# A fused attention and feed-forward kernel: linear-attention and expert weights split in the attention groups and kept in DRAM, all second butterfly stages on GpSimd

## The reference, cut to what matters

```python
x = x + xattn(layernorm(x), ctx, wq, wk, wv, wo, ...)     # 4 batches x 4 kv heads = 16 groups
def h_bitlinear(x, w):                                    # the feed-forward: gate, up, down
    return act_quant(fwht(x)) @ weight_quant(w).T         # weights become -1, 0, 1 times mean(|w|)
x = x + h_bitlinear(silu(h_bitlinear(n, w_gate)) * h_bitlinear(n, w_up), w_down)
x = x + linear_attention(layernorm(x), ctx, Wq, Wg, bg, Wkv, Wo)
x = x + experts(layernorm(x), router_gate, expert_gate_up, expert_down)
```

## Time and profile before

| | |
|---|---|
| median of 3 runs | 1307.87 us (1306.95 to 1311.53) |
| the profiled execution | 1307.24 us, of which the span of the trace is 1305.4 us |
| PE busy | 1194.1 us (91%) |
| DVE busy | 1017.2 us (78%) |
| ACT busy | 839.2 us (64%) |
| POOL busy | 796.9 us (61%) |
| transfers | 157.06 MB, 120 GB/s on average |
| chain that ended last | PE 71%, DVE 13%, DMA 5%, POOL 4%, ACT 3% |

### The profile page before, as it was taken

The page is one execution under the profiler, slowest core; times in us unless marked ns, Lnnn a source line. Parts: engine busy times, 40 slices in busy tenths (PEclk is TensorE's granted clock), DMA queues, the critical chain, the costliest instruction groups (busy, mean ns, idle before and its releaser), DMA issues.

```text
span 1305.4 us, 30426 instructions
## 1 busy us (share of the span) xinstructions
PE 1194.1 (91%) x11547; PEld 895.8 (69%) x11547; DVE 1017.2 (78%) x1971; ACT 839.2 (64%) x1920; POOL 796.9 (61%) x1020
## 2 busy tenths in 40 slices
PE   4998699999999999999999999999999775689898
PEld 2554487777777787877777777777778554466557
DVE  6876778888787887878887888888788577796763
ACT  4665577776667777666767676776777463347431
POOL 2775486775858586675858576685858374452100
PEclk9998999999999999999999999999999887799899
DMA  8630268658866767786575857656676967000000
GB/s 285 199 96 1 35 128 153 138 134 149 172 134 132 146 127 144 139 177 145 124 148 119 153 130 142 136 135 134 133 142 130 193 156 166 1 1 1 1 1 33
DMA packets 499938, 157.06 MB, mean 120 GB/s; under 512 B 484801, under 2 KB 493777, under 8 KB 499793
## 3 DMA queue, kind: packets, MB, share of 16 engines
q1 hardware_dynamic: 497664, 147.77, 53.8%
q0 software_dynamic: 2128, 7.35, 2.1%
HBM read 29.12 MB, written 4.33 MB: 26 GB/s over the span
## 4 chain that ended last, share of the span: by engine, by line
PE 71%; DVE 13%; DMA 5%; POOL 4%; issue 3%; ACT 3%; SPq 0%; POOLq 0%; DVEq 0%; ACTq 0%
PE PS L1179 14%; PE PS L1181 13%; PE PS L1180 13%; PE PS L1331 8%; PE PS L1327 7%; PE PS L1328 7%; DVE mx L1684 4%; DMA pT_l<-pl 3%; DVE pl L1704 2%; PE PS L1280 2%; DMA pT_h<-ph 2%; PE PS L693 1%; DMA sin<-in_c_sin 1%; PE PS L668 1%; PE PS L1289 1%
## 5 line engine op out<-in xcount | busy, mean ns | idle before, releaser
L1684 DVE TENSOR_REDUCE mx<-PS 128x1 f32<-128x512 f32 (+2 forms) x512 | 297.0, 622 | 137.0 <-PE PS L1181 135.4
L1327 PE MATMUL PS<-v_h,pT_h 128*128 128x129 f16 (+1 forms) x1856 | 228.6, 223 | 14.0 <-DMA pT_h<-ph 13.9
L1328 PE MATMUL PS<-v_l,pT_h 128*128 128x128 f16 (+1 forms) x1856 | 228.5, 222 | 0.0
L1922 POOL CAST ph<-pr_end 128x705 f16<-128x705 f32 (+1 forms) x128 | 109.2, 853 | 176.0 <-ACT pr_end L1479 170.1
L1327 PEld LDWEIGHTS PS<-v_h,pT_h 128*128 128x128 f16 (+1 forms) x1856 | 184.1, 99 | 18.3 <-DMA pT_h<-ph 15.5
L1179 PE MATMUL PS<-kT_h,qT_h 128*128 128x512 f16 (+2 forms) x512 | 182.4, 356 | 7.3 <-ACT pr L1479 7.3
L1328 PEld LDWEIGHTS PS<-v_l,pT_h 128*128 128x128 f16 (+1 forms) x1856 | 184.3, 99 | 2.5
L1479 ACT ACTIVATE pr<-PS,nb 128x1024 f32<-128x1024 f32 x128 | 143.9, 1124 | 65.3 <-DVE nb L1692 65.2
L1181 PE MATMUL PS<-kT_h,qT_l 128*128 128x512 f16 (+2 forms) x512 | 181.7, 355 | 0.0
L1180 PE MATMUL PS<-kT_l,qT_h 128*128 128x512 f16 (+2 forms) x512 | 181.7, 355 | 0.0
L1704 DVE TENSOR_TENSOR pl<-pr,ph 128x1024 f16<-128x1024 f32 x128 | 173.1, 1353 | 0.0
(11 more groups left out here) (301 smaller groups left out, 2961.7 us busy)
## 6 DMA issues: line engine op xcount, KB each, us to landing
stage<-in_ctxT SPq DMA_DIRECT2D x8, 800.5 KB, 6.8
lanes<-in_w_lanes SPq DMA_DIRECT2D x16, 192.0 KB, 3.7
stage<-in_wq SPq DMA_DIRECT2D x4, 512.0 KB, 3.9
stage<-in_wo SPq DMA_DIRECT2D x4, 512.0 KB, 3.7
pT_h<-ph SPq DMA_TRANSPOSE x128, 3.6
pT_l<-pl SPq DMA_TRANSPOSE x128, 3.6
ctx_kept<-ctx_h SPq DMA_DIRECT2D x2, 800.5 KB, 8.1
ctx_kept<-ctx_l SPq DMA_DIRECT2D x2, 800.5 KB, 8.6
```

Source lines behind the costliest of these rows:

```text
L1327: mm(PS[:, OB, 0:DH + 1], pT_h[0:rows, slot, t, :], v_h[0:rows, par, v, :], start=t == 0, stop=False)
L1328: mm(PS[:, OB, 0:DH], pT_h[0:rows, slot, t, :], v_l[0:rows, par, v, :], start=False, stop=False)
L1684: dve.reduce_max(mx[:, c:c + 1], PS[:, c, 0:cols(u % LT, c)], AX_X).then_inc(mx_part, 1)
L1922: pool.tensor_copy(ph[:, slot, HALF:LAST + w], pr_end[:, 0:BANK + w]).then_inc(pool_hi, 1)
```

## The change

The nine blocks that are split into halves leave the last group. In each of groups 0 to 14 SyncE loads one piece of 512 columns (after unit 3), ACT makes its high half (after unit 4), DVE its low half (after unit 5), and SyncE stores both in DRAM (after unit 7). `lanes` and the piece share one buffer, `relay`, so the lane load moves behind unit 0 of the next group and waits for the stores; the strips are 1093 columns wide instead of 1024, fifteen instead of sixteen. After the last group eight transfers bring the halves back, and `linear_q` and `linear_gate` wait for them. The router's weights are loaded whole and split on DVE. Of the six ternary blocks DVE makes three in units 1 to 3 of the last group and three in the tail (`wu`, `wd`); their loads are spread over the end of group 14 and the last group; the mean is made at the end of group 14 and the start of the last. The first output tile of the last group is projected, and the first half rotated and quantised, ahead of the last `pv` on PE and the last `out_norm` on DVE. All second butterfly stages are GpSimd's (`bp`), and the four tail lists have a new order.

```diff
-LANE_N = FF * D // LANES // NG
+LANE_N = -(-LANE_ALL // (NG - 1))
+KEPT = 512
+PIECE_HI_AT, PIECE_LO_AT = 4, 5
-LAST_JOBS_AT = [[("out", 0), ("out", 1)], [("out", 2), ("out", 3), ("weight", 0), ("weight", 1)], ...
+LAST_JOBS_AT = [[("mean", 1), ("out", 0), ("out", 1)], [("out", 2), ("out", 3)], [], [], [], [], [], []]
+TERNARY_AT = {1: 0, 2: 1, 3: 2}
 TAIL_PE = stages("""
-    tr0:00 tr0:01 rot:00 rot:01 tq:00 tq:01 ga0:00 tr0:10 up0:00 ga0:01 tr0:11 up0:01 rot:10 ga0:02
+    tr0:00 tr0:01 rot:00 rot:01 tq:00 tq:01 ga0:00 up0:00 ga0:01 tr0:10 ga0:02 up0:01 rot:10 tr0:11
...
 TAIL_DVE = stages("""
-    st0:00 st0:01 lo0:00 lo0:01 qm:00 qq:00 st0:10 st0:11 hh:00 lo0:10 hh:01 lo0:11 b2:00 qm:10 hh:02
-    qq:10 hh:03 b2:02 hl0:00 hh:10 ...
+    st0:00 st0:01 lo0:00 lo0:01 qm:00 qq:00 st0:10 wu:00 wd:00 st0:11 hh:00 lo0:10 wd:01 hh:01 lo0:11
+    hh:02 qm:10 hh:03 qq:10 hl0:00 hl0:01 hh:10 ...
 TAIL_POOL = stages("""
-    rs0:00 rs0:01 rs0:10 rs0:11 b1:00 b1:01 bp:01 b1:02 b1:03 bp:03 b1:10 b1:11 bp:11 b1:12 b1:13 bp:13
+    rs0:00 rs0:01 rs0:10 rs0:11 b1:00 bp:00 b1:01 b1:02 bp:01 bp:02 b1:03 b1:10 bp:03 bp:10 b1:11 b1:12
+    bp:11 bp:12 b1:13 bp:13 rs1:00 ...
@@ SyncE
             def group(g, last=False):
                 for u in range(UNITS):
                     turn(g, u)
-                    if u == LANE_AT + 3 and not last:
+                    if u == 0 and 0 < g < NG - 1:
+                        lane_load(g)
+                    if u == LANE_AT + 1 and g < NG - 1:
                         sp.wait_ge(lane_sum, g + 1)
-                        sp.dma_start(lanes[:, 1:], w_lanes[:, ds((g + 1) * LANE_N, LANE_N)]).then_inc(lane_in, 16)
+                        sp.dma_start(piece_f.rearrange(...), kept_sources[g]).then_inc(pw_in, 16)
+                    if u == UNITS - 1 and g < NG - 1:
+                        sp.wait_ge(pw_lo, g + 1)
+                        for k, t in enumerate((piece_h, piece_l)):
+                            sp.dma_start(kept_w[k, :, g * KEPT:(g + 1) * KEPT], t).then_inc(pw_kept, 16)
+            def lane_load(g):
+                n = lane_width(g)
+                wait(sp, pw_kept, 32 * g)
+                sp.dma_start(lanes[:, 1:1 + n], w_lanes[:, g * LANE_N:g * LANE_N + n]).then_inc(lane_in, 16)
+            def bring_weights():
+                sp.wait_ge(pw_kept, 32 * (NG - 1))
+                ...
+                        sp.dma_start(t, kept_w[k, :, at * KEPT:(at + n) * KEPT]).then_inc(pw_back, 16)
@@ PE, last group, ahead of the last pv; then after it
                         turn(0, 0, 0)
                         turn(0, 0, 1)
+                        wait_bank(pe, ("out", 2), NG - 2)
+                        out_proj(0, NG - 1, job_bank(("out", 0)))
+                        pe.wait_ge(tw_const, 64)
+                        rotate(0, 0)
+                        rotate(0, 1)
                     pv(g, u, par)
...
-            pe.wait_ge(tw_lo, NTL)
             pe.wait_ge(tw_made, 1)
-            for n, (kind, i) in enumerate(OUT_JOBS):
...
+            turn_first(0, 0)
+            turn_first(0, 1)
+            for i, before in ((1, (("out", 3), NG - 2)), (2, (("out", 0), NG - 1)), (3, (("out", 1), NG - 1))):
+                wait_bank(pe, *before)
+                out_proj(i, NG - 1, job_bank(("out", i)))
             tail()
@@ ACT and DVE, each group but the last
+            def weight_piece_hi(g):
+                act.wait_ge(pw_in, 16 * (g + 1))
+                copy(piece_h, piece_f, WS).then_inc(pw_hi, 1)
+            def weight_piece_lo(g):
+                dve.wait_ge(pw_hi, g + 1)
+                dve.scalar_tensor_tensor(piece_l, piece_f, WS, piece_h, ALU.mult, ALU.subtract).then_inc(pw_lo, 1)
@@ DVE, last group
+                    if last and u == UNITS - 1:
+                        lo_part(0, 0, 0)
+                        lo_part(0, 0, 1)
+                        out_lo_part(0, NG - 1, job_bank(("out", 0)))
+                        quantise(0, True)
+                        quantise(0, False)
+                    out_norm(g, u)
+                    if last and u in TERNARY_AT:
+                        ternary(TERNARY_AT[u], tern, tw_made_ternary)
@@ GpSimd
-                    for i in range(STAGES):
-                        weight_load(i)
+                    if g == NG - 2 and u == UNITS - 2:
+                        pool.wait_ge(kq_lo, NG * KQ_STEPS)
+                        ternary_load(0)
+                    if g == NG - 2 and u == UNITS - 1:
+                        ternary_load(1)
+                    if last and u == 0:
+                        ternary_load(2)
...
+                    if last and u == 2:
+                        ternary_load(3)
+                    if last and u in (4, 5):
+                        ternary_load(u)
@@ PE in the tail
             def up_first(hf, j):
+                if j == 0:
+                    pe.wait_ge(tl["wu"], nth("wu", 0, 0))
             def down_first(hf, j):
+                pe.wait_ge(tl["wd"], nth("wd", 0, 1))
             def linear_q(hf, k):
+                pe.wait_ge(pw_back, 128)
```

291 lines of the change are left out of this document (134 added, 157 removed).

## The result

| | before | changed |
|---|---|---|
| median, runs made side by side | 1309.82 us, 7 runs (1306.95 to 1313.3) | 1298.98 us, 7 runs (1296.92 to 1302.97) |
| ratio | | 0.9922, 95% interval 0.9906 to 0.9938 |
| the profiled execution | 1307.24 us, span 1305.4 | 1299.34 us, span 1297.5 |

The changed kernel is 10.8 us (0.8%) faster; forecast were 24. The direction held, the size did not. A second batch gave 1298.44 us and 0.9917 [0.9891, 0.9944].

What follows compares the result with a forecast made beforehand. PE was taken to bound the groups and the end from 1194. Last group 31, less 2 seam, 2 middle and 3 groups, end 0, gave 24 us off 1307.24: 1283.2, as a median 1284; range 1266 to 1300.

Steps and rivals of the forecast that it cites:

- Bound and groups: Groups 0 to 14: a group ends when PE ends; the added work loses 3 us, bounds 0 and 8.
- the two `bring_back`: In the two groups with the return of kept context, the piece load adds to an existing wait: 2 x 1 us.
- Rival (d): Every group loses before unit 0's low turn: PE stands 2.3 us in each of 15, 34.5 us, 1315; chance 0.08.
- The last group: Nine blocks leave it, DVE ends last, and the first quantised tile is turned 31 us earlier, bounds 22 and 33.
- the sum behind it: Last group: DVE 51.9 us busy, transfers 48, 2 us for starts and waits, then 8.6 to rotate and quantise.
- The seam: First quantised turn to `hh:00`: DVE's 4.80 us idle covers `wu` and `wd:00`, projections are not covered; 2 to 3 us lost.
- the butterflies' surplus: 1124 to 1162: four second stages, 11.9 us, leave DVE and `wd:01` comes, 2.0; 9.9 us can be done earlier.
- rival (a): POOL and DVE hold each other up: each of 16 butterfly stages takes 0.6 us more, 9 us, 1293; chance 0.14.
- the projections: Two projections of the last output tile stand ahead of `ga0` on PE, not covered: 2 to 3 us lost.
- Butterflies: From `hh:00`: POOL's chain without gaps, last butterfly after 46 us, not 38.5; 2 us lost, bounds 7 lost and 3 won.
- The end: From 1194 PE is the bound with the same work: 0, bounds 2 lost and 5 won by the new order.
- the forecast's own range: Whole kernel: 1275 to 1292 around the forecast of 1284, chance 0.50.

Runs made afterwards that it cites:

- D: Second butterfly stages of tiles 0 and 2 on DVE, as in the kernel before; with the old order and ternaries in the last group, 1294.18 us, 0.9883.
- P: All second butterfly stages on GpSimd; put alone on the kernel before 1312.67 us, 1.0009; with the old order and ternaries in the last group 1301.27 us, 0.9931.
- the fourth: Changed kernel, old order, ternaries in the last group: all second stages on GpSimd 1301.27 us, tiles 0 and 2 on DVE 1294.18 us.
- shared halves: Changed kernel with second stages of tiles 0 and 2 back on DVE: new order 1301.88 us, 0.9928; old order 1295.80 us, 0.9878.

## Why the prediction was right and wrong

**Bound and groups: right.** Middle groups stayed 57.9 us apart. The 3 us were 4.7, of it 2.7 and 0.8 behind the two `bring_back` (forecast 2 x 1) and 0.9 in the first group. Rival (d) did not occur.

**The last group: the size right, two terms off against each other.** 31 us forecast, 30.4 and, in the second trace of the changed kernel, 29.6 measured (24 to 30.5 in all fifteen with this last group). PE's waits for high turns fell from 11.1 us to 5.1, as they should if the crowded SyncE queue and the loads had made them. But the sum behind it did not come true. The 51.8 us of DVE in the stretch above hold 6.6 of the low halves and `quantise`, which I had counted apart; up to 1084.8, where SyncE issues the return of the weights, it reads:

```profile
1029.90:1084.80 54.90, 42.35 (x465) 32.83 (x464) 45.20 (x93) 25.09 (x34) 22.09 (x30) 0.94 0.99 195
```

DVE was busy 45.2 us, not 51.9, and not full; the transfers, summed at 48 us, took a share of 0.99 of 54.9, that is 54. I had said that DVE ends last. In this stretch the chain that ended last lay for a third of the time in turns, 13.6% and 12.8% in those of `pT_h` and `pT_l` in flight and 7.1% in the issue of the high ones. That the number came out was luck in part: 6.7 us too much of DVE stood for waits that I had put at 2. The last of them is 4.39 us:

```profile
1080.57 0.29 PE L1365 MATMUL PS<-v_h,pT_h 128*128 128x129 f16 x1 [4.39 <-DMA pT_h<-ph]
```

**The seam: the step that failed first.** I had costed `wu:00` and `wd:00` at nothing, because DVE idles 4.80 us ahead of `hh:00`, and `wd:01` at 2.0 us inside the butterflies' surplus. Left out, the three are worth 4.7 us of the kernel. Two faults. The idle time was read in a kernel where PE turned and projected its last output tiles ahead of the first `qi`; in the changed kernel that work stands behind it, DVE idles 3.4 us for it first, and the ternary steps are queued behind that idle time and not in it. And `wd:01` was priced from a row in which GpSimd was quiet. PE met the first fault too, in `up0:00`; the row of its waits from 1093 to 1106:

```profile
PE PS L663 <- DVE wu L1791: 2.6, 1, 2.6
```

`hh:00` followed the statistics on DVE without idle time, so it was DVE's queue that set it. My own rival (a) carried the lock between DVE and GpSimd, but I had charged it to the butterflies alone.

For the projections I had 2 to 3 us ahead of `hh:00`. With the ternaries in the last group the ends give 192.6 against 190.0 (D) and 196.0 against 194.2 us (P), 2 to 3 us. But `hh:00` then ended 7.8 us after the first `qi`, where before had 8.5, and with the ternaries left out in the old order the end is 6.4 us over before's. The amount fits two pairs, the place does not.

**Butterflies: right in size, wrong in mechanism.** 2 us lost were forecast; the move by itself cost 0.7, -0.3 and -2.9 us in three pairs, and 7.1 in the fourth. The last butterfly came 49.1 us after `hh:00`, not 46, with a hole of 6.45 us that I had excluded: GpSimd waited for gated tiles there and was not the bound of this kernel. Sixteen stages are 49.1 - 6.45 = 42.7 us, below my 45.9. Rival (a) did not decide the time, but its mechanism is real: 3.67 to 6.96 us in one small instruction, in three of fourteen traces.

**The end: the second step that failed.** I gave the new order nothing (2 lost to 5 won) and no reason. It costs 8.4 us on the kernel before and 6.1 in the changed kernel with shared halves, both clear of noise, and 3 in the changed kernel itself, which is not. The loss lies behind `hh:13`, where I had expected no change: PE has two waits there, 5.0 us, that the old order does not have.

**The sum again.** Forecast gain 24; less 4.7 for the ternaries, about 3 for the order, 1 to 2 for the groups and 1 for the last group, and with the 2 of the butterflies given back, it is 15 to 16. The measured 10.8 to 12.6 leave 3 to 5 us that are not assigned. That is within the error of the two large terms together (about 4 us); with the ternaries out and the old order the end from the first `qi` is still 196.4 us, 6.4 over before's, and I have no run that separates the rest. The range, 1266 to 1300, held the time at its far end; the forecast's own range did not.

The kernel with kept halves, the old order and shared second stages (1295.8 us, 0.9878 [0.9856, 0.9900]) is 3 to 6 us faster than the changed kernel; with the ternaries in the last group and D (1294.18 us, 0.9883) it is as good. No kernel seen that leaves nothing out is clearly better than these two.

## What to carry to other kernels

An idle time of an engine covers a moved step only if the step is queued ahead of that idle time in the new kernel, and if everything queued behind it can also wait: list each neighbour, and price the step by a row in which the same engines are at work. A new order of in-order queues is an edit with a price of its own, to be measured apart by putting it on the old kernel. A sum that comes out right is still to be compared term by term. Before a product is pulled forward, look at what PE will do in the wait that it used to fill.

## What the runs showed of the hardware

DVE and GpSimd made each other's single instructions 70 to 80% longer (2.17 against 1.28 us, 2.25 against 1.26), while a DVE instruction with an operand in PSUM took the same 1.27 us. A DVE instruction on 128x2 numbers took 0.26 to 1.31 us in seventeen traces and 3.67, 5.35 and 6.96 us in three, beside three to six GpSimd instructions of 1.29 us without a pause. The granted clock fell to 0.67 in a stretch where PE was busy 11.2 of 20 us, so the lost cover was paid twice, in idle time and in a slower engine. Single executions of one kernel differed by up to 13 us (1299.74 to 1313.0) and single traces by 6 us in one cut, of which that small instruction was 5.1; 2 us could only be told by many runs, or by a cut in the trace.
